# Two transformer layers in one kernel: the second norm moves into the first attention loop, the gating writes the second layer's transposed inputs, and the second layer's queries and keys are projected ahead of its loop and fetched

## The reference

```python
x = layernorm(x + attention0(x))      # 16 heads of 8, LoRA on q and v, biases
x = layernorm(x + moe(x))             # 8 experts, top 2; an expert above its capacity is dropped whole
x = layernorm(x + attention1(x))      # 16 heads of 8, rotary positions, causal
x = layernorm(x + spline_ffn(x))      # then gamma and beta

def moe(x):
    probs = softmax(x @ gate_w.T)
    counts = tokens that have the expert in their top 2
    keep = counts <= cap              # cap = int(1.25 * 8192 / 8)
    ...                               # contributions of kept experts alone
```

## Time and profile before

| | |
|---|---|
| three timed runs, median | 1361.35 us (1359.0 to 1361.97) |
| profiled execution, its own time | 1361.33 us |
| its span, first to last instruction | 1359.6 us |
| busy share of the span: PE, DVE, ACT, POOL | 80%, 76%, 61%, 43% |
| mean granted TensorE clock | 0.89 of full speed |
| DMA moved | 137.33 MB, 101 GB/s on average |

### The profile page before, as it was taken

One profiled execution on the slowest core, in us unless ns is written; L12 is line 12 of the kernel. 1 busy time (PEld: TensorE's weight loads), 2 busy tenths in 40 slices (PEclk: granted clock), 3 DMA queues, 4 the chain that ended last, 5 costly groups with the idle time before them and its releaser, 6 DMA issues. The chain is left out here.

```text
span 1359.6 us, 36441 instructions
## 1 busy us (share of the span) xinstructions
PE 1081.3 (80%) x11411; PEld 799.5 (59%) x11411; DVE 1029.6 (76%) x2823; ACT 835.7 (61%) x1904; POOL 582.8 (43%) x696
## 2 busy tenths in 40 slices
PE   2699999999999996516999999999999996501330
PEld 1366666666666663314888888888888873201220
DVE  3578888888888883824787788877888763698885
ACT  1267777777777774552666776767767664401675
POOL 3234434444444432434555555555555506000776
PEclk9799999999999998756999999999999998855555
DMA  2655555565556540305444554444554412100011
GB/s 57 151 122 136 131 139 128 133 140 131 136 135 137 135 100 10 115 29 134 120 119 121 119 123 120 116 121 119 124 119 120 115 35 82 43 0 0 24 47 54
DMA packets 122613, 137.33 MB, mean 101 GB/s; under 512 B 12562, under 2 KB 110258, under 8 KB 113330
## 3 DMA queue, kind: packets, MB, share of 16 engines
q1 hardware_dynamic: 121506, 136.50, 40.6%
q10 hardware_dynamic: 1040, 0.00, 0.0%
HBM read 85.03 MB, written 37.75 MB: 90 GB/s over the span
## 5 line engine op out<-in xcount | busy, mean ns | idle before, releaser
L376 DVE TENSOR_REDUCE attn_negmax<-attn_row_ps 128x2 f32<-128x512 f32 (+1 forms) x1024 | 597.8, 618 | 151.4 <-PE attn_row_ps L558 136.4
L317 ACT ACTIVATE attn_probs<-attn_col_ps 128x512 f32<-128x512 f32 (+1 forms) x1024 | 534.9, 546 | 111.8 <-PE attn_col_ps L580 106.5
L558 PE MATMUL attn_row_ps<-k_st,q_st 72*128 72x256 bf16 (+1 forms) x2048 | 370.3, 263 | 14.9 <-DMA k_st<-attn_scratch 13.9
L580 PE MATMUL attn_col_ps<-q_st,k_st 74*128 74x256 bf16 (+1 forms) x2048 | 369.8, 262 | 2.6 <-ACT attn_probs L317 2.0
L597 PE MATMUL attn_out_ps<-attn_probs,v_sb 128*32 128x256 f32 (+1 forms) x4096 | 230.4, 358 | 0.7 <-ACT attn_probs L317 0.7
L580 PEld LDWEIGHTS attn_col_ps<-q_st,k_st 74*128 74x128 bf16 x2048 | 184.3, 99 | 73.9 <-ACT attn_probs L317 23.2
L558 PEld LDWEIGHTS attn_row_ps<-k_st,q_st 72*128 72x128 bf16 x2048 | 201.9, 99 | 41.3 <-issue 15.3
L597 PEld LDWEIGHTS attn_out_ps<-attn_probs,v_sb 128*32 128x32 f32 x4096 | 123.3, 110 | 71.2 <-issue 21.3
L554 PE MATMUL attn_row_ps<-mask_qk,ident_h 128*128 128x256 bf16 x512 | 141.5, 276 | 19.1 <-DMA k_st<-attn_scratch 18.0
L576 PE MATMUL attn_col_ps<-mask_kq,ident_h 128*128 128x256 bf16 x512 | 141.3, 276 | 1.2 <-ACT attn_probs L317 1.0
L289 POOL TENSOR_SCALAR attn_var<-attn_mv 128x2 f32<-128x2 f32 x64 | 14.3, 223 | 265.8 <-DVE attn_mv L439 265.8
(11 more groups left out here) (230 smaller groups left out, 1689.0 us busy)
## 6 DMA issues: line engine op xcount, KB each, us to landing
q_st<-attn_scratch SPq DMA_DIRECT2D x192, 192.0 KB
k_st<-attn_scratch SPq DMA_DIRECT2D x192, 192.0 KB
attn_scratch<-attn_parts SPq DMA_DIRECT2D x64, 384.0 KB, 2.8
attn_scratch<-attn_parts SPq DMA_DIRECT2D x64, 128.0 KB, 2.9
x_in<-in_L_attn_x_dram SPq DMA_DIRECT2D x32, 128.0 KB, 2.6
x_all<-in_L_attn_x_dram SPq DMA_DIRECT2D x32, 128.0 KB, 7.0
moe_xs<-x_all SPq DMA_DIRECT2D x8, 512.0 KB, 2.9
x_in<-x_mid SPq DMA_DIRECT2D x32, 128.0 KB, 2.4
```

Source lines behind the costliest of these rows:

```text
L317: nc.scalar.activation(probs_of(st, 3, u)[:, j, 0:W], col_ps[:, n % 2, 0:W], ACT.Exp, scale=scale).then_inc(probs_kept, 1)
L376: nc.vector.tensor_reduce(negmax[:, t, 2 * p:2 * p + 2], row_ps[:, row_bank(st, u), 0:2 * keys].rearrange("p (a k) -> p a k", a=2), AX_X, ...
L558: last = nc.tensor.matmul(bank[:, a * keys:(a + 1) * keys], q_st[0:KROWS, sl, h, t * P:(t + 1) * P], k_st[0:KROWS, sl, h, 0:keys], start=n ...
L580: last = nc.tensor.matmul(bank[:, t * N:(t + 1) * N - first], k_st[0:rows, sl, h, t * P:(t + 1) * P], q_st[0:rows, sl, h, first:N], start= ...
```

## The change

1. **In attn0** POOL goes on after the first norm. The variance of a normed row is var·rstd², so the second norm's factor `r_mid` is (var·rstd² + eps)^-0.5: four instructions on 128 by 2 values, and one pass over 256 columns that writes `x_mid`. DVE's statistics, POOL's powers and the 64 normalising instructions leave the moe stage.
2. **In moe** PE transposes `x_mid` where it lies, and ACT copies the transposes to `xT_all`, which is the space of `x_all`, for all 32 batches. ACT takes over the copy of the logits. DVE's routing is done in two halves of 32 tiles, each with one more instruction, since the logits are now those of the second norm's input times `r_mid` and are multiplied by `r_inv` first. The first half can begin when four groups are done.
3. **In attn1** there is no `transpose_x` and no `project_qk` in the steps. 20 batches are projected ahead of the steps, into the two `col_ps` banks, and 12 in step 2, one at the head of each of its first 12 units. ACT copies batches 0 to 2 straight to `qk` and `q_half`; the other 29 go to `probs` (not in use yet) and from there, four at a time, by ACT's own DMA queue to DRAM. In the steps SP fetches `xT` (128 KB), and after the stacked parts `qk` (256 KB) and `q_half` (two halves, 256 KB in all), one step ahead of POOL. `project_v` no longer waits for ACT's copy of q and k. `qk` and `q_half` have three slots instead of one. `dve_v` goes from 4 to 5.

```diff
@@ attention, sync
+            def load_xT(st):
+                if st.has(3):
+                    sp.wait_ge(v_ready, st.seq(3, c=1))
+                sp.dma_start(xT[:, st.slot(0), :], xT_all[:, bass.ds(st.seq(0), 1), :].rearrange("p b n -> p (b n)"))\
+                    .then_inc(x_loaded[st.slot(0)], 16)
+            def load_qk(st):
+                sp.wait_ge(rest_kept, st.seq(2, c=1))
+                if not st.loop:
+                    for n, (first, _) in enumerate(STORED):
+                        if st.off == DEPTH - 1 or first == st.off + 1:
+                            sp.wait_ge(front_stored[n], 16)
+                sl = st.slot(-1)
+                of = qk_dram[bass.ds(st.seq(-1), 1)].rearrange("b p n -> (b p) n")
+                sp.dma_start(qk[:, sl, :, :].rearrange("p s n -> p (s n)"), of).then_inc(qk_loaded[sl], 16)
+                for to, of_row in ((0, P // 2), (P // 2, 0)):
+                    sp.dma_start(q_half[to:to + P // 2, sl, :, :].rearrange("p s n -> p (s n)"),
+                                 of[of_row:of_row + P // 2, :]).then_inc(qk_loaded[sl], 16)
@@ attention, gpsimd
-                    pool.wait_ge(qk_kept, st.seq(0, QKOPS, QKOPS))
+                    if not fronted:
+                        pool.wait_ge(qk_kept, st.seq(0, QKOPS, QKOPS))
+                    elif st.loop or st.off >= SLOTS:
+                        pool.wait_ge(qk_loaded[st.slot(0)], st.turn(0, 16 * QK_LOADS, -16 * QK_LOADS))
+                    else:
+                        pool.wait_ge(front_kept, kept_by(st.off))
...
+                        nc.gpsimd.tensor_tensor(square[:, :], rstd[:, :], rstd[:, :], ALU.mult).then_inc(again, 1)
...
+                        nc.gpsimd.tensor_tensor(mem["x_mid"][:, bass.ds(st.seq(4, TB), TB), :],
+                                                x_all[:, bass.ds(st.seq(4, TB), TB), :],
+                                                r_mid.unsqueeze(2).broadcast_to([P, TB, C]), ALU.mult)\
+                            .then_inc(again, 1)
@@ attention, scalar
+            def front(b):
+                act.wait_ge(front_ready, b + 1)
+                of = col_ps[:, b % 2, :]
+                if b < SLOTS:
+                    nc.scalar.copy(qk[:, b, :, :].rearrange("p s n -> p (s n)"), of).then_inc(front_kept, 1)
+                    for to, of_row in ((0, P // 2), (P // 2, 0)):
+                        nc.scalar.copy(q_half[to:to + P // 2, b, :, :].rearrange("p s n -> p (s n)"),
+                                       of[of_row:of_row + P // 2, :]).then_inc(front_kept, 1)
+                    return
+                if b - SLOTS >= 4 * PROBS:
+                    act.wait_ge(front_stored[(b - SLOTS - 4 * PROBS) // FRONT_GROUP], 16)
+                nc.scalar.copy(staged(b), of).then_inc(front_kept, 1)
+                group = (b - SLOTS) // FRONT_GROUP
+                first, to = STORED[group]
+                if b + 1 == to:
+                    act.wait_ge(front_kept, kept_by(b))
+                    n = (first - SLOTS) // 4 % PROBS
+                    act.dma_start(qk_dram[first:to].rearrange("b p n -> p b n"), probs[:, n, 0:to - first, :])\
+                        .then_inc(front_stored[group], 16)
+                            if fronted and not st.loop and st.off == 3:
+                                for stored in front_stored:
+                                    act.wait_ge(stored, 16)
@@ attention, tensor
-                if st.has(0):
+                if fronted:
+                    pe.wait_ge(x_loaded[st.slot(2)], st.turn(2))
+                if st.has(0) and not fronted:
                     pe.wait_ge(qk_kept, st.seq(0, QKOPS, QKOPS))
+            def front(b):
+                if b >= 2:
+                    pe.wait_ge(front_kept, kept_by(b - 2))
+                for s in range(2):
+                    last = nc.tensor.matmul(col_ps[:, b % 2, s * N:(s + 1) * N], wqk[:, s, :], xT_all[:, b, :],
+                                            start=True, stop=True)
+                last.then_inc(front_ready, 1)
+                    if fronted and not st.loop and st.off == 2 and FRONT_EARLY + n < B:
+                        front(FRONT_EARLY + n)
@@ moe, vector
-                    if st.has(0):
-                        measure(dve, st, st.seq(0), 0)
...
+                def route(half):
+                    tiles = slice(half * HALF, (half + 1) * HALF)
...
+                    dve.wait_ge(logits_kept, GROUPS // 2 * (half + 1))
+                    then(nc.vector.tensor_tensor(logits_, logits_, over_experts(r_inv[:, tiles]), ALU.mult))
...
+                route(0)
+                route(1)
```

More of the change, by code:

```diff
@@ L180, in attention, with kept_by, staged @@
         UNITS, ROW_BANKS = NH * TB, 3
+        STORED = [(b, min(b + FRONT_GROUP, B)) for b in range(SLOTS, B, FRONT_GROUP)]
+        QK_LOADS = 3
+        def kept_by(b):
+            return 3 * SLOTS + b - SLOTS + 1 if b >= SLOTS else 3 * (b + 1)
+        def staged(b):
+            n = (b - SLOTS) % (4 * PROBS)
+            return probs[:, n // 4, n % 4, :]
         def probs_of(st, lag, u):
@@ L217, in step @@
                                 .then_inc(stacked[sl], 16)
-                if st.has(2) and x_dram is not None:
+                if fronted and st.has(-1) and (st.loop or st.off >= AHEAD):
+                    load_qk(st)
+                if st.has(2) and not fronted:
                     sp.dma_start(x_all[:, bass.ds(st.seq(2, TB), TB), :],
@@ L331, in step @@
                     for s in range(2):
-                        if n == at["act_qk"][s] and st.has(0):
+                        if not fronted and n == at["act_qk"][s] and st.has(0):
                             if s == 0:
@@ L362, in step @@
                             .then_inc(mT_kept, 1)
+            if fronted:
+                for b in range(FRONT_EARLY):
+                    front(b)
             pipeline(act, step)
@@ L609, in step @@
                         score_rows(st, n)
-                    if n == at["pe_xT"] and st.has(0):
+                    if not fronted and n == at["pe_xT"] and st.has(0):
                         transpose_x(st)
@@ L616, in step @@
                             sum_values(st, lag, u)
-                    if n == at["pe_qk"] and st.has(0):
+                    if not fronted and n == at["pe_qk"] and st.has(0):
                         project_qk(st)
@@ L640, with groups @@
 GROUPS = TILES // GT
-LN_SPLIT = 6
+HALF = TILES // 2
 MT = 4
-def groups(eng, step):
-    pipeline(eng, step, 2, 4, GROUPS, 0)
+def groups(step):
+    for n in range(GROUPS + 3):
+        step(Step(0, n, 2, GROUPS))
 def moe(nc, mem, w):
-    x_all, x_mid, ident = mem["x_all"], mem["x_mid"], mem["ident"]
+    x_all, x_mid, xT_all, r_mid, ident = (mem[k] for k in ("x_all", "x_mid", "xT_all", "r_mid", "ident"))
+    xT_flat = xT_all[:, :, :].rearrange("p b n -> p (b n)")
     with ExitStack() as ctx:
@@ L809, in step @@
                         last.then_inc(logits_ready, 1)
[L811 to L814 removed]
+                groups(step)
+                for half in range(2):
+                    pe.wait_ge(routed, COUNTED * (half + 1))
+                    last = nc.tensor.matmul(g_ps[:, 0, 0:E], ones[:, :], counts[:, half, :], start=half == 0,
+                                            stop=half == 1)
+                last.then_inc(counts_ready, 1)
             @block.scalar
             def _(act):
[L818 removed]
+                act.wait_ge(consts, E + 2)
                 act.dma_start(gate_T[:, 0:E], w["L0_ffn_gate_w"].rearrange("e c -> c e"),
@@ L835, in step, with weigh @@
                         nc.scalar.copy(gates_sb[:, j, :], g_ps[:, j, 0:2 * P]).then_inc(gates_kept, 1)
-                groups(act, step)
-                act.wait_ge(shifted, 1)
-                nc.scalar.activation(probs[:, :, :], left[:, :, :], ACT.Exp).then_inc(exp_kept, 1)
-                act.wait_ge(scaled, 2)
-                with act.Fori(0, LN_SPLIT) as i:
-                    for t in range(GT):
-                        tile = bass.ds(i * GT + t, 1)
-                        nc.scalar.activation(x_mid[:, tile, :].rearrange("p t c -> p (t c)"),
-                                             x_all[:, tile, :].rearrange("p t c -> p (t c)"), ACT.Identity,
-                                             bias=shift[:, tile], scale=rstd[:, tile]).then_inc(ln_kept, 1)
+                    if st.has(2):
+                        g, j = st.off - 2, st.slot(2)
+                        act.wait_ge(logits_ready, st.seq(2, c=1))
+                        of = l_ps[:, j, 0:2 * P].rearrange("p (t g m) -> p t g m", t=2, m=32)
+                        nc.scalar.copy(logits[:, g * GT:(g + 1) * GT, :].rearrange("p (g t) e -> p t g e", t=2),
+                                       of[:, :, :, 0:E]).then_inc(logits_kept, 1)
+                        if g == GROUPS // 2:
+                            weigh(0)
+                def weigh(half):
+                    act.wait_ge(shifted, 3 * half + 1)
```

(4 more changed lines are left out.)

265 lines of the change are left out of this document (131 added, 134 removed).

## The result

The changed kernel takes 1407.8 us (1403.5 to 1412.17) against 1360.88 us: the ratio is 1.0346, 95% interval 1.0312 to 1.0381. It is slower by 47 us, where the prediction had 1342.4 us and a gain of 19: the time lies above its range and on the other side. The profiled execution has a span of 1405.2 us against 1359.6.

A forecast was written before the change was run, and what follows sets the result against it. PE at full clock was taken to bound attn1's loop, 15.43 us a step. From 1361.33 us: +2.4 (attn0), -14.5 (moe), +5.4 (attn1's ramp), -12.2 (27 steps) = 1342.4 us; range 1330 to 1354.

The forecast's parts named there:

- Moe: Moe stage: with the norm gone and routing in two halves it lasts 35.0 us, -14.5 us.
- Attn0's tail: End of attn0: POOL's five added instructions, hidden in the loop, are uncovered after the last step, +2.4 us.
- The ramp: Attn1's start until step 5: first scores at 31.4 us, a slower step 2, sum 80.9 against 75.5, +5.4 us.
- PE's saving and the bound by DVE's chain: Attn1's loop: PE loses 1.6 us a step, but DVE's norm and maxima hold the step at 14.28, gain 1.15.
- The place of the collision: Attn1's loop: POOL's first rotary pass starts just when DVE's norm application (L444) is released, in the changed steps.
- The step that failed: Attn1's loop: both pieces of DVE's norm application wait for one POOL pass of 1.28 us, ending before POOL's next instruction.
- forecast slip of 0.7 us: Attn1's loop: delay of DVE's norm application by POOL's first pass, 1.28 - 0.60 = 0.7 us a step, charged whole.
- rival that POOL gets in between: Attn1's loop: POOL's second pass precedes the norm's second piece; slip 2.1, step 16.4 us, in all 1380; chance 0.20.
- prediction's own sign of being wrong: Attn1's loop: among the signs listed, L444 taking 2.5 us or more, with a period above 15.9 us.
- Hidden: Attn1's loop: the new DMAs, 512 KB more a step, cost nothing at a share of 0.49, asked for one step ahead.
- The point from which the change is slower than before: Attn1's loop: the whole change loses from a slip of 1.40 us a step on.

The follow-up runs named there:

- alone: Kernel before with only parts 1 and 2 of the change (second norm on POOL in attn0, new moe stage), attn1 as before: 1345.54 us, ratio 0.9892.
- e3_fill: Changed kernel with four matmuls of unused result on PE ahead of unit 3's rows in each loop step, collision left in: 1382.22 us, ratio 1.0149.
- e9_gate_early: Kernel of e1_gate with SP's fetch of q and k moved to the step's start, right behind xT: 1323.45 us, ratio 0.9732.
- e2_gap: Changed kernel with one wait between POOL's first and second rotary pass, for the end of the first: 1420.1 us, ratio 1.046.
- e1_gate: Changed kernel in which POOL's first rotary pass also waits until DVE has written x_mid: 1349.05 us, ratio 0.9928.
- e12_early_alone: Changed kernel with the fetch of q and k at the step's start, POOL's passes still meeting the norm's application: 1406.14 us, ratio 1.034.
- e6_ln_pool_m_act: Changed kernel with attn1's norm applied by POOL instead of DVE and the small DMA of maxima on ACT's queue: 1351.92 us, ratio 0.9936.
- e7_before_2_passes: Kernel before with two more POOL passes, results unread, behind L291 in attn1's projecting steps: 1384.28 us, ratio 1.0175.
- e8_one_pass_m_act: Changed kernel with the small DMA on ACT's queue and POOL's wait for x_mid between its two rotary passes: 1364.62 us, ratio 1.0034.

## Why the prediction was wrong

- **Moe: right.** Forecast 35.0 us and -14.5, measured 34.8 and -14.7; alone, -14.
- **Attn0's tail: right in kind.** Forecast +2.4; the end came 1.6 us later. The five instructions took 2.6 us behind L354, but that instruction itself stood 1.1 us earlier than L301 before. In the loop they cost nothing: 27 of its steps take 14.69 us each before and 14.71 after.
- **The ramp: right, a little small.** First scores 29.8 us in (31.4 forecast); until the loop +7.1 instead of +5.4.
- **PE's saving and the bound by DVE's chain: right.** The step free of the collision and the burst is 14.37 us (forecast 14.28), and 13.81 once the norm is off DVE.
- **The place of the collision: right.** It is where the text put it, in every step, and with what it does to PE's clock it is the whole loss of the loop.
- **The step that failed: "blocked, they have been issued and end right behind the pass, as L1738 did, ahead of POOL's next instruction".** They did not. Each piece waited for a pass of its own: 1.29 us a piece, 2.50 for both. The forecast slip of 0.7 us was 1.9 in L540, which brought the steps at full clock to 16.2 us (e3_fill), 1.85 above the 14.37 of e9_gate_early. L1738, a copy of 16 rows beside a memset, didn't show what the text took from it: it ended at 7.57, when POOL's next instruction had already begun (7.55). What was needed was two DVE instructions in a row beside two POOL passes, and the trace before had them, right behind the quoted L1164 (rows below). L1164 ended behind one pass (L271, at 27.66), and L1165 began 0.03 us after the next and ended behind that one too (29.02 against 28.90). The rival that POOL gets in between was this one, with its 2.1 us, and had 0.20. The Trainium skill's rule (SBUF — State Buffer, who interferes with whom: whoever issues first holds the shared port pair for the whole instruction) agrees with the rows in which POOL's pass began first. Two DVE instructions waited although the traces have them begin first: L1164 (27.01 against 27.04) and the second piece in e2_gap (835.70 against 835.77). The rule says nothing of who goes next when both wait; here POOL's next pass did, in e2_gap even with 0.07 us between the passes. The prediction's own sign of being wrong, L444 at 2.5 us or more and a period above 15.9, is what came.
- **What no case had: the clock.** A slip of 1.9 us alone would have made 27 x (16.22 - 15.44) = +21 us in the steps, 1376 us or so in all. The other 27 x 1.15 = 31 us come from PE's clock, which fell to half behind the stall of 2.3 us in 17 of 27 steps, and e3_fill shows that it's the standstill that brings this. The rival's 1380 lacked it as much as the forecast, and so did the upper end of the range.
- **"Hidden" was said of the fetches, and is true only beside the collision.** The sum was right (a share of 0.49 leaves room), the place wasn't looked at: 512 KB behind the stacks make one burst of some 8 us, at whose end the 8 KB stand for which PE waits. That costs 15.20 - 14.37 = 0.83 us a step in e1_gate (two steps at a lower clock among them) and nothing in the changed kernel (e12_early_alone).
- The point from which the change is slower than before was put at a slip of 1.40 us a step. E3_fill, at 1.85 and full clock in 24 steps, is slower, as that point would have it: by 22 us, where 27 x (1.85 - 1.40) would give 12.

The rows of the trace before that answer to the failed step:

```profile
27.74 1.15 POOL L276 TENSOR_TENSOR attn_rest<-attn_qk,attn_parts 128x512 f32<-128x512 f32 x1
...
27.77 1.24 DVE L1165 CAST table_hm<-table 128x193 bf16<-128x193 f32 x1
```

Not settled: why POOL's waiting pass goes ahead of DVE's second piece, where at the start of the program two DVE copies both ended before the next memset did (one difference the traces show: there the second copy had started 1.2 us before POOL's instruction ended, while L540's second piece starts at 785.53, 0.05 us after POOL's second pass); and why the clock falls behind some stalls of 2.3 us and not behind others of the same length in the same loop.

## What to carry to other kernels

When an input comes earlier, ask what its consumer did while it waited for it: here POOL's idle time had kept its passes away from the norm's application, the one DVE instruction on the chain that leads to the row maxima that they held up, and the gain of 1.1 us a step turned into a loss of 1.9. Of an instruction in n pieces beside n passes of another engine, price the case in which each piece waits for a pass. Before a stall is given a price, look in the traces for what the granted clock did behind others of its length; and a transfer is hidden by where it stands in the step, not by the mean share of the DMA engines.

## What the runs showed of the hardware that was not expected

The granted clock fell to half behind single standstills of PE in an otherwise full loop: behind 2.25 us in the step shown (0.56 over the next 3.9 us), and in e1_gate behind one of 1.77 us, after which a step took 18.97 us where most took some 15. PE's timeline and the window behind it, in e1_gate:

```profile
703.96 0.39 PE L676 MATMUL attn_col_ps<-mask_kq,ident_h 128*128 128x256 bf16 x1 [1.77 <-DMA q_st<-attn_mT_sb]
```

```profile
703.96:708.00 4.04, 4.04 (x28) 3.02 (x32) 2.15 (x5) 1.32 (x4) 3.18 (x4) 0.50 0.15 47
```

It came again in e1_gate behind a stall of 2.11 us (the next step 17.65 us, mean clock 0.90) and in e6_ln_pool_m_act behind one of 1.80 us (17.72 us, 0.90). The stalls of about 1.1 us in e7_before_2_passes and of 1.3 us in e8_one_pass_m_act (24.7 us in 19 steps) left it at 1.00 in all steps. An 8 KB DMA took 4.2 to 5.8 us from its issue to PE's release, 4.9 on average, behind the burst of the fetches, on either of two queues.
